# A two-layer transformer step on one core: where the first layer drains, the order of the second layer's first operations, of POOL's row transfers and of SP's queue is changed

## The reference, cut to what matters

```python
# layer 0
xn = layernorm(x)
s = windowed_attention(xn, w_attn) @ w_proj.T    # 16 heads of 8, window of 64, rotary
g = silu(xn @ ternary(w).T * alpha + bias)
x = x + s * g
# layer 1
xn = layernorm(x)
q, k, v = split(xn @ W_in.T)
Tq, Tk = chebyshev(clip(q)), chebyshev(clip(k))  # order 5 of T, 16 heads of 8
num = (Tq * beta * cumsum(Tk * v)).sum();  den = (Tq.sum() * beta * cumsum(Tk.sum())).sum()
s = (num / den) @ W_out.T
logits = xn @ router_w.T + router_b              # 8 experts, the best 2 of each row
y = sum over its 2 experts of cw * (gelu(xn @ w1[e].T + b1[e]) @ w2[e].T + b2[e])
x = x + s * silu(layernorm(y + xn))
```

## Time and profile before

| | |
|---|---|
| median of 3 runs | 874.4 us (871.69 to 875.07) |
| the profiled execution, its own time | 876.45 us |
| its span, from the first instruction to the last | 874.6 us |
| PE busy | 596.5 us, 68% |
| DVE busy | 660.3 us, 75% |
| ACT busy | 441.9 us, 51% |
| POOL busy | 436.9 us, 50% |
| mean granted clock of PE | 0.847 of full speed |
| indirect transfers xbuf<-x,slots (L492) | 64, 65.2 us on POOL |

### The profile page before, as it was taken

The page is one execution under the profiler, slowest core; times in us unless marked ns, Lnnn a source line. Parts: engine busy times, 40 slices in busy tenths (PEclk is TensorE's granted clock), DMA queues, the critical chain, the costliest instruction groups (busy, mean ns, idle before and its releaser), DMA issues.

```text
span 874.6 us, 22303 instructions
## 1 busy us (share of the span) xinstructions
PE 596.5 (68%) x7049; PEld 402.2 (46%) x7049; DVE 660.3 (75%) x1711; ACT 441.9 (51%) x1075; POOL 436.9 (50%) x697
## 2 busy tenths in 40 slices
PE   1898899998988988842327777777777775324220
PEld 0566666665655655520214555555555553112110
DVE  4688888888787677743845898899898898617777
ACT  1456555554544454410417787888888774101111
POOL 3145555555457677657703344444444343764721
PEclk9999999998999799965658999999999997555555
DMA  9999999200000000001121232323232321111211
GB/s 228 345 283 287 286 288 287 75 0 0 0 8 18 15 18 18 16 13 45 48 76 38 85 99 93 102 81 104 85 100 85 96 69 41 52 45 36 66 31 36
DMA packets 127372, 80.93 MB, mean 93 GB/s; under 512 B 11832, under 2 KB 118208, under 8 KB 127296
## 3 DMA queue, kind: packets, MB, share of 16 engines
q1 hardware_dynamic: 122160, 70.97, 27.2%
q0 software_dynamic: 5136, 9.02, 3.8%
HBM read 18.85 MB, written 49.55 MB: 78 GB/s over the span
## 4 chain that ended last, share of the span: by engine, by line
PE 34%; DVE 33%; issue 17%; POOL 7%; ACT 4%; SPq 1%; DVEq 1%; DMA 1%; another core or an unknown queue 1%; POOLq 0%; ACTq 0%
PE m_ps L1047 5%; PE e_ps L1059 4%; DVE yts L1394 3%; POOL experts_sb L563 3%; DVE mneg L1142 3%; PE y_ps L1010 2%; PE q_ps L954 2%; PE m_ps L823 2%; PE p_ps L1003 2%; DVE pr L1391 2%; PE y_ps L887 2%; DVE pr L1393 2%; ACT pexp L610 2%; DVE rot L1184 2%; PE m_ps L837 2%
## 5 line engine op out<-in xcount | busy, mean ns | idle before, releaser
L610 ACT ACTIVATE pexp<-e_ps 128x512 f32<-128x512 f32 x128 | 76.5, 598 | 75.4 <-PE e_ps L870 66.7
L1142 DVE TENSOR_REDUCE mneg<-m_ps 128x4 bf16<-128x512 f32 x128 | 84.7, 683 | 22.5 <-PE m_ps L837 22.2
L1047 PE MATMUL m_ps<-xs,wb 128*128 128x512 f16 x276 | 80.4, 403 | 19.8 <-issue 18.6
L563 POOL DMA_INDIRECT experts_sb<-ybuf,slots x64 | 63.5, 993 | 32.3 <-issue 18.9
L492 POOL DMA_INDIRECT xbuf<-x,slots x64 | 65.2, 1019 | 16.6 <-issue 14.9
L1019 PE MATMUL p_ps<-eye_sb,yn 128*128 128x128 f32 x32 | 11.6, 363 | 80.4 <-DVE yn L1399 64.2
L887 PE MATMUL y_ps<-pexp,vd 128*32 128x128 f32 x512 | 57.6, 295 | 3.1 <-ACT pexp L610 1.0
L557 POOL TENSOR_TENSOR pexp<-rot,pexp 128x512 f16<-128x512 f32 x24 | 27.8, 1157 | 56.6 <-ACT pexp L731 56.6
L851 PE MATMUL e_ps<-early 128*128 128x256 bf16 x256 | 52.0, 284 | 0.1
L557 POOL TENSOR_TENSOR pexp<-qt,pexp 128x512 f16<-128x512 f32 x24 | 30.3, 1264 | 43.1 <-ACT pexp L731 43.1
L1101 PE MATMUL e_ps<-b_sb,cwt 8*128 8x128 f32 x64 | 16.6, 436 | 49.3 <-ACT cwt L780 49.3
(11 more groups left out here) (223 smaller groups left out, 2129.7 us busy)
## 6 DMA issues: line engine op xcount, KB each, us to landing
xbuf<-zero_sb SPq DMA_DIRECT2D x71, 256.0 KB, 4.0
ybuf<-zero_sb SPq DMA_DIRECT2D x71, 256.0 KB, 3.6
wb<-experts_sb SPq DMA_DIRECT2D x46, 256.0 KB, 2.3
xs<-xbuf SPq DMA_DIRECT2D x23, 256.0 KB, 2.7
ybuf<-vd SPq DMA_DIRECT2D x23, 256.0 KB, 2.2
experts_sb<-in_experts_w SPq DMA_DIRECT2D x8, 512.0 KB, 6.9
x_all<-in_x SPq DMA_DIRECT2D x8, 256.0 KB, 5.3
xbuf<-x,slots POOLq DMA_INDIRECT x64
```

Source lines behind the costliest of these rows:

```text
L563: nc.gpsimd.indirect_dma_start(yg[:, 2 * (B * n + b) + k, :], None, ybuf, bass.IndirectOffsetOnAxis(ap=slots[:, k, B * n + b:B * n + b + 1 ...
L610: nc.scalar.activation(pexp[:, j, :, :], e_ps[j % 2][:, :, :], ACT.Exp, scale=float(D) ** -0.5).then_inc(exp_ready.sem, 1)
L1047: last = nc.tensor.matmul(u_ps[f % 2], wb1[:, i % 2, f, a, :], xg16[:, i % 2, b, :], start=k == 0, stop=k == len(PARTS) - 1)
L1142: nc.vector.tensor_reduce(mneg[:, n.batch, j // 2, (j % 2) * NG:(j % 2) * NG + NG], m_ps[j % 2][:, :, :], AX.X, ALU.max, negate=True).then ...
```

## The change

POOL's step takes one number, rows, and sends them as its last act; steps 24 to 31 send 4, 3, 4, 3, 4, 3, 4, 3, steps 35 and 36 send 3 each, and the last 30 follow step 37. SP calls load_up(0), load_down(0), carry_row(0), load_up(1), load_down(1), carry_row(1), then waits for the scatters, load_rows(0), load_rows(1), carry_row(2). In the drain PE calls project(0) at the end of step 35, ACT v_copy(0) at the end of step 36 and DVE clip(0) at the end of step 36. project(1), clip(1) and cheb_keys(0) come ahead of or between the router's operations for the last group; owners() stands in c = 0 ahead of cheb_out(0), and weights_of_two() in c = 1. ACT scales w_in between its steps 7 and 8, in the first layer. The functions themselves compute what they did.

```diff
@@ SP
-            for c in range(LEAD - 1):
-                carry_row(c)
             weights_split.wait(sp, Tile(TAUS - 1, 3))
             sp.wait_ge(s_owner, 1)
             sp.wait_ge(s_y_zeroed, 16 * BLOCKS)
             for i in range(2):
                 load_up(i)
                 load_down(i)
+                carry_row(i)
             sp.wait_ge(s_scattered, 16 * 2 * NT)
             load_rows(0)
             load_rows(1)
+            for c in range(2, LEAD - 1):
+                carry_row(c)
@@ POOL
-            def step(head, first=0, second=0):
+            def step(head, rows=0):
...
                     nc.gpsimd.tensor_copy(vd[:, n.batch, 0, :, :], vd[:, n.batch, 2, :, :]).then_inc(values_kept.sem, 1)
-                    send(first)
...
                     nc.gpsimd.tensor_copy(w16[:, blocks, :, :], split_sb[:, :, :, :]).then_inc(weights_split.sem, 1)
-                    send(second)
...
+                send(rows)
...
             for n in range(8):
-                step(Tile(6, n), 2, 1)
-            step(Tile(TAUS, 0), 2, 1)
-            step(Tile(TAUS, 1), 0, 1)
-            step(Tile(TAUS, 2))
-            step(Tile(TAUS, 3))
-            send(10)
-            step(Tile(TAUS, 4))
-            send(6)
-            step(Tile(TAUS, 5))
+                step(Tile(6, n), 4 - n % 2)
+            for n in range(6):
+                step(Tile(TAUS, n), 3 if 3 <= n < 5 else 0)
             send(2 * NT - sent[0])
@@ ACT
-            pipeline(act, step, 6)
-
+            for n in range(8):
+                step(Tile(0, n))
             act.wait_ge(s_late_weights, 16 * 9)
             nc.scalar.mul(w_in[:, 0:2 * C], w_in[:, 0:2 * C], INV * R1).then_inc(s_scaled, 1)
-            act.wait_ge(s_chosen, 3)
-            nc.scalar.activation(rs[:, 5, :], rs[:, 4, :], ACT.Exp).then_inc(s_route_exp, 1)
-            act.wait_ge(s_late_weights, 16 * 9)
-            weighted.wait(act, Tile(TAUS, 0))
-            values_kept.wait(act, Tile(TAUS, 0))
+            with act.Fori(2, TAUS) as t:
+                for k in range(4):
+                    step(Tile(t, k))
...
-            v_copy(0)
+            for n in range(6):
+                step(Tile(TAUS, n))
+                if n == 4:
+                    v_copy(0)
+            polynomials(0)
             v_copy(1)
-            polynomials(0)
             polynomials(1)
+            act.wait_ge(s_chosen, 3)
+            nc.scalar.activation(rs[:, 5, :], rs[:, 4, :], ACT.Exp).then_inc(s_route_exp, 1)
+            weighted.wait(act, Tile(TAUS, 0))
+            values_kept.wait(act, Tile(TAUS, 0))
@@ PE
-            for n in range(6):
-                step(Tile(TAUS, n))
-                if n == 2:
-                    count(1)
-            logits_ready.wait(pe, Tile(TAUS, 0))
-            count(2)
-            pe.wait_ge(s_counts_read, 3)
...
-            pe.wait_ge(s_late_weights, 16 * 9)
-            pe.wait_ge(s_scaled, 1)
-            project(0)
+            for n in range(6):
+                step(Tile(TAUS, n))
+                if n == 2:
+                    count(1)
+                if n == 3:
+                    gate_steps.wait(pe, Tile(TAUS, -1), 2)
+                    pe.wait_ge(s_late_weights, 16 * 9)
+                    pe.wait_ge(s_scaled, 1)
+                    project(0)
             project(1)
+            logits_ready.wait(pe, Tile(TAUS, 0))
+            count(2)
+            pe.wait_ge(s_counts_read, 3)
@@ DVE
-            for n in range(6):
-                step(Tile(TAUS, n))
-                if n == 1:
-                    choose(1)
-                if n == 2:
-                    place(1)
-            choose(2)
-            place(2)
-            owners()
...
-            clip(0)
+            for n in range(6):
+                step(Tile(TAUS, n))
+                if n == 1:
+                    choose(1)
+                if n == 2:
+                    place(1)
+                if n == 4:
+                    clip(0)
             clip(1)
+            choose(2)
             cheb_keys(0)
+            place(2)
             for c in range(NT):
                 if c + 1 < NT:
                     cheb_keys(c + 1)
                 if c + 2 < NT:
                     clip(c + 2)
+                if c == 0:
+                    owners()
                 cheb_out(c)
-                if c == 0:
+                if c == 1:
                     weights_of_two()
```

More of the change, by code:

```diff
@@ L90, in wait @@
         engine.wait_ge(self.sem, tile.count(self.per, k))
-def pipeline(engine, step, lags):
-    for n in range(8):
-        step(Tile(0, n))
-    with engine.Fori(2, TAUS) as t:
-        for k in range(4):
-            step(Tile(t, k))
-    for n in range(lags):
-        step(Tile(TAUS, n))
 def keys_steps(c):
```

## The result

The changed kernel takes 889.17 us (median of four runs, 887.9 to 890.1) beside 874.74 us of the kernel before on the same chip: a ratio of 1.0167, interval 1.0133 to 1.0201. It is slower by 14 us; I had forecast 18 us faster. The profiled execution has a span of 888.3 us against 874.6.

A forecast was written before the change was run, and what follows sets the result against it. The prediction took POOL's transfer queue, then SP's queue order, to hold the start of the passes; 15.4 us from SP's order plus 2.5 from the steps made 17.9, so median 856.5 us from 874.4, range 850.5 to 866.

The forecast's parts named there:

- SP's order: SP's queue before pass 0: with weights issued ahead, rows reach PE at 442.3 instead of 457.69, 15.4 us earlier.
- POOL's total in the drain: Between the layers: the same 36 transfers and two steps, so the scatter does not end earlier by the new split.
- Chebyshev inside the drain: First Chebyshev operations moved into the drain: they fill idle holes, cost nothing; PE and DVE have 8 us to spare.
- Transfers at the end of POOL's step: Steps 24 to 31, four and three transfers: 0.2 us a step saved, 2.5 us with step 32, bounds -1 and +8.
- The 0.9 us set for step 32: Saving claimed for POOL's step 32, which loses its transfers; part of the 2.5 us forecast for the steps.
- The signs that I had named for being wrong: Weights or a copy last before pass 0's rows, transfers ending later than 437, or steps longer than 12 us.
- Rival (b): End of POOL's step is the wrong place: 1 us a step lost, gain 7, median 867 us; chance 9%.
- Rival (d): Slower: DVE starved beside transfers as beside the second layer's gathers, owners late; two such stretches give median 883 us; 4%.
- The rule on the shared port: Skill page: GpSimd cannot write descriptors while DVE holds their port pair; 36 transfers would end over 100 us later.

The follow-up runs named there:

- the rows-sooner version: Changed kernel with three separated single transfers a step and only pass 0's weights ahead of the rows: 846.32 us (0.9871) on the third chip, 857.16 us (0.9783) on the fourth.

## Why the prediction was wrong

**SP's order: the right term, its size in part by luck.** 15.4 us were forecast, 14.7 measured alone. But at the start of pass 0 the profiles show only 11.6 of them (448.63 against the 460.21 of the first profile) and 13.3 with Chebyshev's part (446.95); the rest is a part behind it that took 411.4 us in place of 414.4, which nothing here explains. Beside the transfers SP's instructions start 0.7 us apart or more, so it did not wait "at the scatter some 10 us before it lands"; with Chebyshev's part the rows reached PE at 444.43, not 442.3. In the changed kernel it was worse: the owners come from DVE at 437.4, SP issues pass 1's down weights only at 463.23 and the rows at 466.92 (timeline of SP):

```profile
463.23 0.70 SPq L412 DMA_DIRECT2D wb<-experts_sb  x1
...
466.92 1.60 SPq L418 DMA_DIRECT2D xs<-xbuf  x2
```

**POOL's total in the drain: right.** 36 transfers and two steps took 50.0 us before and 49.8 after (412.57 to 462.35), but started 25.7 us later.

**Chebyshev inside the drain: nil, right in the sum and wrong in its cover.** DVE's wait for POOL's rstd is 2.6 us in place of 11.8, as forecast ("about 3"), and PE's for the rows 11.9 in place of 15.2 (waits of DVE and of PE, kernel after):

```profile
DVE early L1140 <- POOL rstd L537: 2.6, 1, 2.6
```

```profile
PE t_ps L1014 <- DMA xs<-xbuf: 11.9, 1, 11.9
```

But DVE did not have 8 us to spare: between 447.6 and 459.6 its operations of 0.2 to 0.4 us start 1.4 us apart in most cases, beside the run of 30 transfers, and the trace records DVE's own updates there 0.9 to 1.2 us late.

**Transfers at the end of POOL's step: the step that failed.** I had set four or three transfers against POOL's 3.55 us of idle time and got 10.9 us a step at best and "11.9 to 12.0 a step: nothing saved, or 1 us lost" at worst. Measured: 14.9, and 15.4 to 15.5 on the three other chips on which it ran, alone or with the rest; a loss of 24 to 29 us in the place of a gain of 2.5. The sum counted what POOL does and when. The runs show that this was next to no cost at that place (88.9 us with POOL kept nearly as busy by powers), and that the cost came through another term, which the sum did not have: signals from PE that arrive late, most of them only behind the run of transfers. The 0.9 us set for step 32 did not come either; the stretch behind its value copy grew by 1.7. The signs that I had named for being wrong were both there, steps longer than 12 us and transfers that end later than 437 (462.35). Rival (b), the end of the step is the wrong place, has the place but prices it at 1 us a step; measured it is 3.0 to 3.6.

**Rival (d) had half of it.** I had seen that DVE stands still beside the gathers, "waits for nothing that the profile names", and asked only what that would do to the owners. Most likely it was the same thing, a signal that comes late beside a run of indirect transfers (in the rows-sooner version it was, with 9.9 us), and the right question was which signals cross the eight steps. Against it I counted DVE's busy time beside Chebyshev, which says nothing of signals.

**The rule on the shared port.** In the kernel after, the 64 transfers last 0.96 to 1.23 us, with a median of 0.96 as before, also beside DVE's work. Starved descriptor writes, of which the Trainium skill speaks (SBUF — State Buffer, "A bandwidth-pool intuition that's wrong"), are not what happened here; this trace does not show them either. It is the other engines that wait beside the transfers, not the transfers beside them.

**Open.** What in the chip delays the signals, whether it is the making of the descriptors or the transfers that they start, and why one chip of five did not show it, no run here can tell; nor was the change run there. Since matmul ends are modelled, the trace can't tell a late signal from a matmul whose last step is held up; ACT waits in either case.

## What to carry to other kernels

Do not price a GpSimd indirect transfer by the time it takes on POOL alone: look at the waits that the profile puts to "remote" beside it, and ask which signals other engines send each other meanwhile. Keep such transfers single, with one of POOL's other instructions between them, at a place with slack behind it; a run belongs where nobody else has anything to pass on. And measure on more than one chip before a rule is made of it.

## What the runs showed of the hardware

- On four of five chips, PE's semaphore updates that fell beside a run of back-to-back indirect transfers came late: up to 1.3, 2.5, 3.8 and 5.1 us in runs of 1, 2, 3 and 4, most of them 0.2 to 1.2 us behind the end of the run. One power of 0.57 us behind each transfer brought this to 1.1 us at most.
- Runs of 1, 2, 3, 4 at the end of a step made the step 0.2, 1.7 to 3.1, 3.3 and 5.5 us longer there (pairs of one execution each, PE's clock included). Powers of one column that keep POOL busy 4.3 and 3.2 us in that place cost 0.2 to 0.5 us a step.
- On those chips SP's register loads, moves and DMA issues started about 0.7 or 1.4 us apart beside the transfers, and DVE's short dependent operations 1.4 us apart beside a run of 30.
- On the remaining one, the third chip of the experiments, no update of PE was more than 0.2 us late. The same kernel took 94.4 us in place of 114.8 for the eight steps, SP's instructions for two passes 8 us where they took 19 on a chip with late updates, and the kernel before 858.8 us in place of 875 to 877 as a whole.
